# A gated cross-attention block with a five-matrix FFN on one core: the FFN weights in SBUF start 128 bytes off a multiple of 512

## The reference, cut to what matters

```
x = x + tanh(g_xattn) * attention(layernorm(x), ctx, ctx)        # Wq, Wk, Wv, Wo, bo
n = layernorm(x)
h = silu((n @ w1.T) * s1) * ((n @ w2.T) * s2)                    # 256 -> 1024, twice
h = gelu((h @ h1.T) * h1s)                                       # 1024 -> 1024
h = gelu((h @ h2.T) * h2s)                                       # 1024 -> 1024
x = x + tanh(g_ffn) * ((h @ w3.T) * s3)                          # 1024 -> 256
```

## Time and profile before

| | |
|---|---|
| time, median of 3 runs | 1783.74 us (1782.88 to 1784.28) |
| time of the profiled execution | 1783.53 us |
| its span (first to last instruction) | 1781.2 us |
| TensorE matmuls busy | 1721.5 us, 97% of the span, 11078 instructions |
| VectorE, ScalarE, GpSimd busy | 1319.0, 1310.2, 1098.3 us (74%, 74%, 62%) |
| mean granted clock of TensorE | 0.985 |

### The profile page before, as it was taken

How to read it: one execution, slowest core, us unless ns; L and a number is a source line. 1 busy time by engine, 2 the same in 40 slices (tenths; PEclk the granted TensorE clock), 3 DMA queues, 4 the chain that set the end, 5 groups by cost and what they waited for, 6 DMA issues and landing times.

```text
span 1781.2 us, 39684 instructions
## 1 busy us (share of the span) xinstructions
PE 1721.5 (97%) x11078; PEld 1471.0 (83%) x11078; DVE 1319.0 (74%) x2803; ACT 1310.2 (74%) x3022; POOL 1098.3 (62%) x1647
## 2 busy tenths in 40 slices
PE   4599999999999999999999999999999999999998
PEld 3488888888888888888888888888888888888886
DVE  4877777777777777777777778777787777777763
ACT  3778777778777778777777777777777777777773
POOL 3567656667656667656657655656755656765652
PEclk7699999999999999999999999999999999999999
DMA  8644444444444544444544444444344454444420
GB/s 298 202 121 112 121 130 135 141 131 113 115 135 130 147 132 114 114 132 131 142 143 111 118 127 135 137 141 115 115 123 135 135 141 121 115 124 130 118 60 7
DMA packets 362523, 229.29 MB, mean 129 GB/s; under 512 B 274688, under 2 KB 332288, under 8 KB 360960
## 3 DMA queue, kind: packets, MB, share of 16 engines
q1 hardware_dynamic: 360336, 217.14, 43.4%
q10 hardware_dynamic: 2160, 11.81, 1.7%
HBM read 113.53 MB, written 41.94 MB: 87 GB/s over the span
## 4 chain that ended last, share of the span: by engine, by line
PE 92%; issue 2%; DMA 1%; DVE 1%; ACT 1%; POOL 1%; SPq 1%; POOLq 0%; ACTq 0%; DVEq 0%
PE ffn L984 71%; PE work L924 13%; PE s_bank L959 3%; PE pv L975 3%; PE work L1064 2%; SPq L357 0%; DMA q_saved<-q_parts 0%; DMA aw<-in_attn_w 0%; DMA xT<-in_x_T 0%; POOL hb L516 0%; ACT probs L824 0%; SPq L361 0%; DMA k_saved<-k_parts 0%; DVE full L654 0%; POOL ha L511 0%
## 5 line engine op out<-in xcount | busy, mean ns | idle before, releaser
L984 PE MATMUL ffn<-hb,W 128*128 128x512 f32 x2048 | 504.3, 399 | 1.3 <-POOL hb L516 1.3
L661 DVE TENSOR_REDUCE full<-ffn 128x256 f32<-128x512 f32 x512 | 349.5, 688 | 180.1 <-PE ffn L984 175.7
L984 PE MATMUL ffn<-ha,W 128*128 128x512 f32 x2048 | 479.9, 391 | 1.2 <-POOL ha L511 1.2
L984 PEld LDWEIGHTS ffn<-ha,W 128*128 128x128 f32 x2048 | 378.0, 188 | 80.9 <-POOL ha L511 2.4
L984 PEld LDWEIGHTS ffn<-hb,W 128*128 128x128 f32 x2048 | 375.2, 188 | 82.1 <-POOL hb L516 8.8
L824 ACT ACTIVATE probs<-probs,exp_bias 128x128 f32<-128x128 f32 x1024 | 320.3, 390 | 42.6 <-POOL exp_bias L479 41.5
L471 POOL TENSOR_TENSOR p_parts<-probs,p_parts 128x512 f16<-128x512 f32 x256 | 299.1, 1168 | 20.5
L984 PE MATMUL ffn<-x2T_hi,W 128*128 128x256 f32 x1024 | 260.2, 290 | 1.0 <-DVE x2T_lo L757 0.5
L516 POOL TENSOR_TENSOR hb<-full,hb 128x256 fp32r<-128x256 f32 x256 | 187.8, 739 | 112.4 <-ACT full L842 104.8
L984 PE MATMUL ffn<-x2T_lo,W 128*128 128x256 f32 x1024 | 254.3, 284 | 0.0
L842 ACT ACTIVATE full<-full,cols 128x256 f32<-128x256 f32 x512 | 253.2, 494 | 0.0
(11 more groups left out here) (86 smaller groups left out, 2432.5 us busy)
## 6 DMA issues: line engine op xcount, KB each, us to landing
k<-k_saved SPq DMA_DIRECT2D x256, 128.0 KB, 2.7
q<-q_saved SPq DMA_DIRECT2D x256, 128.0 KB, 2.7
k_saved<-k_parts SPq DMA_DIRECT2D x32, 512.0 KB, 2.9
q_saved<-q_parts SPq DMA_DIRECT2D x32, 512.0 KB, 2.9
wnat<-in_ffn_w ACTq DMA_DIRECT2D x11, 1024.0 KB, 6.4
xT<-in_x_T SPq DMA_DIRECT2D x32, 256.0 KB, 3.3
cT<-in_ctx_T SPq DMA_DIRECT2D x32, 256.0 KB, 3.4
x_in<-in_x SPq DMA_DIRECT2D x32, 256.0 KB, 3.6
```

The lines of the kernel that those rows point to most:

```text
L661: dve.tensor_reduce(full[:, m % 4], src[:].rearrange("p (a t) -> p t a", a=2), AX_X, ALU.add).then_inc(done, 1)
L984: return pe.matmul(dst, w, h, **flags)
```

## The change

Two tiles are added that nothing reads or writes. HALF is 64 and BANK 512, so `first_part` has 32 columns (128 bytes) and `second_part` 480 columns (1920 bytes). W now begins at 14336 + 128 = 14464. Every tile behind W moves up by 128 + 1920 = 2048 bytes, and so stays on a multiple of 2048; the last ends at 227328. No instruction is added, removed or moved.

```diff
         to_boundary = sb("to_boundary", [P, TO_BOUNDARY])

+        first_part = sb("first_part", [P, HALF // 2])
         W = sb("W", [P, W_COLS], F32R)
+        second_part = sb("second_part", [P, BANK - HALF // 2])
         aw = sb("aw", [P, 4, KE, E])
```

## The result

| | before | after |
|---|---|---|
| median time | 1783.55 us (4 runs) | 1794.78 us (1793.87 to 1799.72, 4 runs) |
| ratio, 95% interval | 1 | 1.0071 (1.0058 to 1.0083) |
| span of the profiled execution | 1781.2 us | 1791.9 us |

A forecast was written before the change was run, and what follows sets the result against it. TensorE's matmuls, 97% of the span, were taken to bound the kernel. All terms were 0, so the profiled 1783.53 us stayed 1783.5 and the median forecast was 1783.7 us, range 1780 to 1802.

The forecast's parts named there:

- What bounds the kernel: Whole kernel: TensorE's matmuls cover 97% of the span, so number of matmuls times distance of starts sets the end.
- The fillers: The two added tiles: no engine touches them and no instruction is added; cost 0.
- the move by 2048: All tiles behind W keep their place relative to powers of two up to 2048; taken as 0.
- ScalarE's writes: ScalarE's 11 roundings write W 128 bytes further on; taken as 0, at most 0.2 us either way.
- The price of a read at 128: TensorE's 7168 reads of W, now crossing multiples of 512: 0 ns each, or 0.5 to 2.5 ns for the range.
- rival A: W's fp32r weight reads at L984: crossing a multiple of 512 holds them up; 1787 to 1802 or 1880 us; chance 0.24.
- Rival B: All W matmuls: the 13.4 ns excess is two streams clashing in step; offset gives 1736 or 1688 us; chance 0.12.
- The rule of two ports: TensorE reads stream and weights through independent ports, so the excess is no address clash; moving W gives neither plus nor minus.

The follow-up runs named there:

- all_2048: One 2048-byte filler before W in the kernel before the change, moving W and every tile behind it by 2048: 1784.02 us, ratio 1.0000.
- micro: TensorE alone, reference's work left out; sections of 64 matmuls differing in offsets, columns or type: 512 columns took 14.67 us aligned, 15.04 or 15.09 at a 128-byte difference.
- micro3: TensorE alone, 64 matmuls a section, offsets alternating between matmuls, also 16-bit operands: 512-column pairs 1.6 and 3.2 ns slower than aligned, 16 bit some 216 ns.
- all_128: One 128-byte filler before W in the kernel before the change, so weights and streams all lie at 128: 1784.29 us, ratio 0.9997.
- w_256: The change with fillers of 256 and 1792 bytes, W 256 past a multiple of 512, against the kernel before: 1784.07 us, ratio 0.9994.
- micro2: TensorE alone, 48 matmuls a section: offsets in 16-byte steps, fewer columns, smaller loads; 256 columns at best 113.3 ns a matmul, 512 never under 226.7.

## Why the prediction was right or wrong

**What bounds the kernel: right.** TensorE's stream is the path; a few ns on each matmul of L984 came out in the time nearly one to one (15.5 us more in L2 and L3, some 3 back in L1; 10.7 in the span).

**The fillers, the move by 2048, ScalarE's writes at 0: right.** all_2048 is at 1.0000, and the rounding of W lasts a median of 1903 ns instead of 1902.

**The price of a read at 128: wrong, and this is the step that failed.** The prediction put it as "I take **0 ns** per read, from mean_of". It measured (489.7 - 479.9)/2048 = 4.8 ns per matmul in L2, (510.0 - 504.3)/2048 = 2.8 in L3 and about -1 in L1. mean_of and ident were the wrong neighbours because they are float32: micro shows no such cost for float32 at 128 bytes, and micro3 none for 16 bit at 64 and 128. Of the types tried only fp32r has the effect. The prediction named this doubt under rival A and gave it too little weight, although its own rows set fp32r apart: 13.5 ns of excess against 2.6. It also took the place of one operand as the variable, where all_128 shows that the place of both counts. That alone did not mislead it: mean_of and ident too lie off their partners, which begin on multiples of 512.

**Rival A: the size was right by luck and the mechanism wrong.** The time of 1795 is in its 1787 to 1802, and so in the range. But its 0.5 to 2.5 ns a read were met in no part of L1 to L3: the sum came out there because a larger loss in L2 and L3 stood against a gain in L1. And nothing is held up by crossing a multiple of 512: all_128 and w_256 cross and cost nothing. Its mark, "L1's loads become longer than 192 ns", did not appear; they became 188.

**Rival B: the right kind of mechanism and, for most matmuls, the wrong sign.** The rate does depend on how weights and stream lie to each other. With 256 columns the offset helps, down to 113.3 ns alone and 116 in L1; with 512 the aligned start is already the best seen. The argument against it, that L2 is even over slices 0, 512, 1024 and 1536 bytes apart, was true and proved too little: it spoke of steps of 512, and with 512 columns the effect has vanished again at 256 already.

**The rule of two ports.** The Trainium skill, "TensorE: Matmul & The Clock Gate", section "Step-by-step: what each phase is for", was taken to mean that the excess cannot hang on addresses. micro, with every other engine idle, shows that for fp32r it does (226.7 against 232.5 to 233.4 ns); the measurement decides. It does not follow that the two ports meet: smaller loads did away with the cost of the offset, but the excess itself grew. What holds up what inside TensorE is not shown.

## What to carry to other kernels

For fp32r matmuls at full rate, keep the stationary and the streamed tile at the same offset modulo 256 bytes when 512 columns stream: that was the best seen, and another offset cost up to 8 ns on 227. With 256 columns a stream at 192 bytes to weights at 0 is worth a trial, since it took 4 ns off 120. For float32 at 128 bytes and for 16 bit at 64 and 128 the placement did not matter. And when a price is taken from a neighbouring row, ask first whether that row has the trait that could carry the cost, here the data type and the excess that it alone shows.

## What the runs showed of the hardware that was not expected

- Aligned fp32r matmuls pay some 13 ns over one column a tick of 2.4 GHz, whether 256, 384 or 512 columns stream (119.8 ns in micro, 173.3 in micro2, where the 48 matmuls of 384 columns take from 559.44 to 567.76 us, and 226.7); float32 pays 2.5 per instruction (215.8), and 16 bit no more than 2.7 (some 216).
- For fp32r the excess moves with the byte offsets of weights and stream: 19 to 21 ns with the weights at 32 to 160 bytes with 512 columns, 6.7 ns at best with 256.
- The offsets do not fix the rate: 256 columns with weights at 64 ran at 117.8 ns in micro ((245.90 - 238.36)/64) and at 113.3 in micro2 with the same offsets, after other sections and on another chip. Which of the two makes the difference is not shown.
- At offset 0 a 128x64 or 128x32 weight load beside the same 512 columns makes the fp32r matmul slower (230 and 232 ns) than a 128x128 one (226.7), and an offset of 128 then costs nothing more. Why is open.
